# Bias rows of messages, projections and outputs: made by TensorE, or added by VectorE

## The chip, the cores and the metric

The kernel runs on one core of a Trainium2 chip. The metric is the device time of one execution in microseconds, and the times shown are medians of several runs. A core has five engines that run their own instruction streams and meet at semaphores: TensorE (PE; matmuls, with weight loads shown apart as PEld), VectorE (DVE), ScalarE (ACT), GpSimd (POOL) and SyncE (SP, which here issues most DMAs).

## The reference

Four graph layers run one after another over 1875 nodes of 256 features and 60000 edges, each with a residual sum and a layer norm: `x = layernorm(x + L(x))`. The first is a relational attention layer with 8 relations and 4 heads. The other three are where the change lies:

- The second layer has, for each of two relations, a two-step message per node, `m = relu(relu(x W_r + b_r) W_r + b_r)`, summed over the edges of that relation, and then one step of a recurrent cell and a three-layer network with biases `b1`, `b2`, `b3`.
- The third layer is two SAGE convolutions in a row. Each projects, `xp = relu(x W_proj + b_proj)`, averages `xp` over the incoming edges, and forms `out = aggr W_l + b_l + x W_r`, whose rows are divided by their norm. Between the two is a relu.
- The fourth is an attention layer with four heads that has no bias.

All is computed in float32.

## The kernel before

The 1875 nodes are held as 15 tiles of 128 rows, the features as 256 columns. The engines' programs are written out by hand, with semaphores named in the code; nothing is planned by a tool, so the order in the source is the order on each engine. The first 1126 us (the first layer) gather and sort edge data and walk over it; the rest is dense work.

Segment sums of messages are dense too: a matrix of edge counts, kept as 16-bit integers (`adjacency`), is cast by ScalarE and VectorE into chunks of float32 and multiplied by TensorE with the messages. To keep precision, a message is split into two halves: ScalarE writes the high half as `relu` of the PSUM bank (`message`, line 735), VectorE writes the low half as `max(bank, 0) - high` from the same bank (`low_half`, line 1360), and only then is the bank free.

A bias that varies along the columns is made by TensorE: the bias is split into three bf16 parts in three partitions (`bias_parts`, lines 1288 to 1305, seven VectorE instructions in a chain), and a matmul of three rows with a matrix of ones writes the bias row to all 128 partitions of the bank, before the matmuls of the data are accumulated on it. There are 105 such matmuls:

- Messages of the second layer (lines 1835 to 1837): ten groups of three tiles, in banks 4, 5 and 6. For each tile one bias matmul and two data matmuls (fp32; each is seen as two passes in the trace, so four passes a tile). Before each group but the first and the last stands the hidden layer of a later group (`hidden`, line 1812, eight passes of 384 columns). A group waits until the low halves of the group before are done (`m_ev`). ScalarE takes the hidden layer's relu (line 745) and the three high halves in turn.
- The last layer of the gate network (lines 1926, 1927): 15 bias matmuls. The bias parts of the next stage are made by VectorE in the second of the five gate rounds, between the statistics and the residual sum (line 1421).
- Projections (`project`, lines 1938 to 1940): 15 tiles for each convolution in four banks, `t % 4`; tile t waits for the low half of tile t - 4 (`p_ev`). The first four tiles of the second convolution are issued in the outputs' tail of the first. In front of the low halves of the second convolution VectorE computes the attention columns of the fourth layer (`attention_columns`, line 1446).
- Outputs (lines 1971 to 1974): 15 tiles for each convolution. For each tile two matmuls with `W_l` into the left half of a bank, one bias matmul and two matmuls with `W_r` into the right half. VectorE then scales the left half by the reciprocal count (line 1476), adds the right half (line 1477) and takes the sum of squares (line 1478). At the end of each group of four tiles it normalises; in the second convolution it also adds to `X` and computes the layer norm (lines 1489, 1309, 1322).

SyncE loads the first bias rows with the relation weights in the walk of the first layer (`first_weights`, line 478), into three partitions. It loads the bias rows of the convolutions when the relations' aggregation is done (line 518), and the six weights of the convolutions when the last matmul of the gate network is done (`x3_mm`, line 521). TensorE waits for all six before the first projection.

## Time and profile before

| | us |
|---|---|
| median of 3 runs | 1721.92 |
| lowest and highest | 1721.28, 1725.96 |
| profiled execution | 1728.33 |
| its span in the profile | 1726.6 |

| engine | busy us | share of the span | instructions |
|---|---|---|---|
| PE | 1377.2 | 80% | 4918 |
| PEld | 774.1 | 45% | 4918 |
| DVE | 1150.2 | 67% | 2944 |
| ACT | 725.8 | 42% | 1258 |
| POOL | 545.8 | 32% | 517 |

The profile is of one execution; times in it count from the start of its span. Busy time of PE is the sum of its matmuls' latencies as far as they don't overlap, so a busy PE need not be PE at its best. PEclk is the TensorE clock that was granted, as a share of full speed; the clock has two levels, 1.2 and 2.4 GHz, so a mean of 0.92 over a stretch means that 16% of it ran at the lower one. A row of the timeline gives the start, the time from the first instruction's start to the last one's end, the engine, the line of the code, what it does and how many instructions were merged; brackets say how long the engine had been idle and what ended the wait.

### The profile page before, as it was taken

Reading aid. Unit: us, or ns where it says so; the run is one execution under the profiler, and the core shown is the slowest. Engines: PE = TensorE matmul, PEld = TensorE weight load, DVE = VectorE, ACT = ScalarE, POOL = GpSimd, SP = SyncE. Lnnn points to the kernel's source line nnn. Section 1 sums busy time; section 2 is a strip of 40 time slices with the busy share of each in tenths; the row PEclk is TensorE's granted clock in tenths of the full one; section 3 lists DMA queues with packets and bytes.
Section 4 is the critical chain, followed back from the end, with each engine's and each line's share of the span. In section 5 each row is a group of like instructions: output and inputs, shape, how many; then the busy total and the mean of one; then the engine's idle time right before and its main releaser. Section 6 shows DMA issues by size and latency. Waiting matters only on the chain.

```text
span 1726.6 us, 21308 instructions
## 1 busy us (share of the span) xinstructions
PE 1377.2 (80%) x4918; PEld 774.1 (45%) x4918; DVE 1150.2 (67%) x2944; ACT 725.8 (42%) x1258; POOL 545.8 (32%) x517
## 2 busy tenths in 40 slices
PE   5897987777777777777169999979999989989930
PEld 2453643411111111112058777745876548758620
DVE  6232544289999999998989998852375443543737
ACT  1233543367777777776000000023595535316022
POOL 0102777777777777775000000000000000000023
PEclk9998555665555555555559999989999989989985
DMA  4534666765555565555148888600000010000023
GB/s 168 153 131 149 210 210 215 214 189 181 188 181 188 178 190 182 185 179 161 48 136 302 265 276 270 212 1 0 0 27 2 1 37 0 2 13 1 2 67 73
DMA packets 84505, 223.88 MB, mean 130 GB/s; under 512 B 18456, under 2 KB 27588, under 8 KB 83908
## 3 DMA queue, kind: packets, MB, share of 16 engines
q1 hardware_dynamic: 60452, 158.01, 26.4%
q0 software_dynamic: 23968, 64.77, 14.3%
q8 instruction: 50, 0.82, 0.2%
q14 instruction: 35, 0.29, 0.1%
HBM read 140.09 MB, written 82.63 MB: 129 GB/s over the span
## 4 chain that ended last, share of the span: by engine, by line
PE 48%; DVE 23%; issue 15%; POOL 6%; DMA 3%; ACT 3%; DVEq 2%; SPq 0%; POOLq 0%; ACTq 0%
PE bank L1786 13%; PE bank L1846 10%; PE bank L1645 6%; POOL arena L601 5%; DVE arena L1172 4%; DVE arena L1173 3%; DVE adjacency L1179 3%; PE bank L1901 2%; PE bank L1940 2%; DVE arena L1214 2%; PE bank L1837 2%; DVE arena L1391 2%; PE bank L1812 2%; PE bank L1974 1%; DVEq L404 1%
## 5 line engine op out<-in xcount | busy, mean ns | idle before, releaser
L601 POOL DMA_INDIRECT arena<-feat_table,arena x469 | 508.6, 1084 | 241.6 <-issue 228.8
L1725 PE MATMUL bank<-arena 128*128 128x480 f16 x586 | 336.1, 574 | 123.4 <-DVE arena L1173 116.5
L683 ACT ACTIVATE arena<-bank 128x480 uint16<-128x480 f32 x586 | 332.7, 572 | 119.1 <-PE bank L1725 112.5
L609 POOL DMA_INDIRECT arena<-al_table,edge_ends x15 | 14.7, 982 | 861.5 <-DMA al_table<-arena 857.2
L1179 DVE TENSOR_TENSOR adjacency<-adjacency,arena 128x480 uint16 x586 | 233.3, 398 | 10.2 <-DVE arena L1192 6.2
L1725 PEld LDWEIGHTS bank<-arena 128*128 128x128 f16 x586 | 60.9, 104 | 398.8 <-DVE arena L1173 307.1
L1786 PE MATMUL bank<-arena 128*128 x966 | 230.0, 393 | 0.8 <-issue 0.3
L1786 PEld LDWEIGHTS bank<-arena 128*128 128x128 f32 x966 | 175.4, 191 | 55.7 <-issue 33.7
L1173 DVE TENSOR_SCALAR arena<-iota,arena 128x480 f16<-128x480 f16 x586 | 196.5, 335 | 0.0
L1270 DVE TENSOR_TENSOR arena<-arena 128x1024 f32<-128x1024 f32 x118 | 139.8, 1212 | 14.6 <-DMA arena<-edge_rows 13.0
L1172 DVE TENSOR_SCALAR arena<-iota,arena 128x128 f16<-128x128 f16 x586 | 144.1, 246 | 0.8 <-ACT adjacency L647 0.8
L1645 PE MATMUL bank<-arena 128*128 128x512 f32 x240 | 111.2, 619 | 5.8 <-ACT arena L632 3.0
L1846 PE MATMUL bank<-count_chunks,message_halves 128*128 128x472 f32 x480 | 103.4, 377 | 2.1 <-DVE message_halves L1360 2.1
L715 ACT ACT_TABLE_LOAD x2 | 2.6, 1283 | 240.3 <-DVE ln_mean_var L1316 240.3
L1846 PEld LDWEIGHTS bank<-count_chunks,message_halves 128*128 128x128 f32 x480 | 90.0, 188 | 15.5 <-issue 2.9
L1688 PE MATMUL bank<-arena 128*128 x588 | 74.9, 189 | 16.4 <-DVE arena L1129 11.1
L781 ACT ACTIVATE count_chunks<-adjacency 128x944 fp32r<-128x944 uint16 (+1 forms) x30 | 69.9, 2334 | 39.7 <-PE bank L1846 39.7
L1688 PEld LDWEIGHTS bank<-arena 128*128 128x128 f16 x588 | 59.6, 105 | 46.4 <-issue 33.3
L1277 DVE TENSOR_TENSOR arena<-iota,arena 128x1024 f32<-128x1024 f16 (+1 forms) x61 | 73.7, 1209 | 9.2 <-PE bank L1786 8.8
L632 ACT ACTIVATE arena<-bank 128x512 f32<-128x512 f32 x60 | 35.8, 597 | 100.5 <-PE bank L1645 96.8
L1674 PE MATMUL bank<-adjacency,ident 128*128 128x512 f16 x128 | 66.3, 617 | 14.6 <-ACT arena L659 11.6
L1645 PEld LDWEIGHTS bank<-arena 128*128 128x128 f32 x240 | 46.9, 200 | 61.6 <-issue 54.4
(311 smaller groups left out, 1725.4 us busy)
## 6 DMA issues: line engine op xcount, KB each, us to landing
arena<-edge_rows SPq DMA_DIRECT2D x117, 520.0 KB, 4.5
edge_rows<-arena SPq DMA_DIRECT2D x67, 520.0 KB, 2.9
edge_rows<-arena SPq DMA_DIRECT2D x67, 390.0 KB, 2.6
feat_table<-arena SPq DMA_DIRECT2D x60, 260.0 KB, 2.1
arena<-feat_table,arena POOLq DMA_INDIRECT x469
arena<-in_w SPq DMA_DIRECT2D x1, 2048.0 KB, 9.8
arena<-in_xT SPq DMA_DIRECT2D x1, 1920.0 KB, 18.3
arena<-in_x SPq DMA_DIRECT2D x1, 1792.0 KB
```

Of the source, the lines that this page charges most:

```text
L601: g.indirect_dma_start(out=PLACE[k][:, t - lo, :], out_offset=None, in_=feat_t, in_offset=bass.IndirectOffsetOnAxis(ap=IE[:, t:t + 1], axi ...
L683: a.activation(EV[st % AS].rearrange("p r k -> p (r k)"), PS[4 + st % 4][:, 0:R2 * KW], ACT.Copy)\
L1172: v.tensor_scalar(OHS[st % AS], iota128[:, :], lo, None, ALU.is_equal)
L1173: v.tensor_scalar(OHK[st % AS], iota480[:, :], key, None, ALU.is_equal).then_inc(s["a_oh"], 1)
L1179: v.tensor_tensor(dst, dst, EV[st % AS], ALU.add).then_inc(s["a_add"], 1)
L1270: v.tensor_tensor(rows, rows, al, ALU.mult).then_inc(s["r_wgt"], 1)
L1277: v.tensor_tensor(OHR[:, i % ORING, 0:n * P].rearrange("p (s j) -> p s j", j=P), iota128[:, :].rearrange("p (a j) -> p a j", a=1).to_broad ...
L1645: ins = mm(PS[c][:, :], XT0[:, k, P * t:P * (t + 1)], W0[:, k, 512 * c:512 * (c + 1)], start=(k == 0), stop=(k == 1))
L1688: ins = mm(PS[4 + g % 2][:, 3 * H * k:3 * H * (k + 1)], KO[g % 3][:, lo:lo + P], ERW[:, bass.ds(offs[k], 3 * H)], start=True, stop=True)
L1725: mm(PS[4 + st % 4][:, 0:R2 * KW], OHS[st % AS], OHK[st % AS], start=True, stop=True).then_inc(s["a_mm"], 1)
L1786: mm(BANKS[:, bass.ds(out_at, D)], OHR[:, (st // RG) % ORING, P * (st % RG):P * (st % RG + 1)], FBf[:, bass.ds(places[st % RK] >> 12, D)], ...
L1846: ins = mm(PS[4 * fo + j0 + j][:, 0:CW], m[:, P * fo:P * (fo + 1)], ch[:, CW * j:CW * (j + 1)], start=start, stop=stop)
```

## The change

The 90 bias matmuls of messages, projections and outputs are left out; the first data matmul starts the accumulation. The bias rows are loaded by broadcast to all 128 partitions in float32. For messages and projections VectorE adds the bias to the bank in place (`add_bias`) as soon as TensorE has finished the tile and signals `biased`; ScalarE waits for that signal in place of TensorE's, and the low half follows as before. VectorE issues its adds ahead of the low half of the tile before. For outputs the bias goes into VectorE's first instruction, which scales the left half and adds the bias in one. The gate network keeps its bias matmuls, so `bias_parts` remains for that one row of 256 columns, and the splitting in the second gate round goes. The four bias rows of the convolutions (128 KB each now) are loaded ahead of the six weights; TensorE waits for all ten.

```diff
             def first_weights():
...
-                for i, b in enumerate((brow[0:1, :], brow[1:2, :], b3)):
-                    sp.dma_start(BROW[0][0:3, D * i:D * (i + 1)], b.broadcast_to([3, D])).then_inc(s["ld_wt1"], 16)
+                for b, to in ((brow[0:1, :], BIAS1[0]), (brow[1:2, :], BIAS1[1]), (b3, BROW[0:3, :])):
+                    sp.dma_start(to, b.broadcast_to([to.shape[0], D])).then_inc(s["ld_wt1"], 16)
...
-            sp.wait_ge(s["chunk_used"], R2 * SH)
-            for i, b in enumerate((bp1, bl1, bp2, bl2)):
-                sp.dma_start(BROW[1][0:3, D * i:D * (i + 1)], b.broadcast_to([3, D])).then_inc(s["ld_b2"], 16)
             sp.wait_ge(s["x3_mm"], NC)
+            for to, b in zip(BIAS2, (bp1, bl1, bp2, bl2)):
+                sp.dma_start(to, b.broadcast_to([P, D])).then_inc(s["ld_wt2"], 16)
             for i, w in enumerate((wp1, wl1, wr1, wp2, wl2, wr2)):
                 sp.dma_start(W2L[i], w.rearrange("(k p) n -> p k n", k=2)).then_inc(s["ld_wt2"], 16)
...
-            def message(n, bank, wide, exact=False):
+            def message(n, bank, wide, exact=False, before=0):
+                act.wait_ge(s["biased"], before + n + 1)
                 dst = WIDE[n] if wide else halves(n)[0] if exact else halves1(n)[0]
                 a.activation(dst, PS[bank][:, 0:D], ACT.Relu).then_inc(s["hi_ready"], 1)
...
+            def add_bias(bank, bias, made, count):
+                dve.wait_ge(made, count)
+                v.tensor_tensor(PS[bank][:, 0:D], PS[bank][:, 0:D], bias, ALU.add).then_inc(s["biased"], 1)
...
-                for n in range(R2 * NT):
-                    low_half(n, halves1(n), 4 + n % 3, s["m_ev"])
+                for n in range(0, R2 * NT, 3):
+                    for j in range(4):
+                        if j < 3:
+                            add_bias(4 + j, BIAS1[n // NT], s["m_mm"], n + j + 1)
+                        if j:
+                            low_half(n + j - 1, halves1(n + j - 1), 4 + j - 1, s["m_ev"])
...
-                if c == 1:
-                    dve.wait_ge(s["ld_b2"], 64)
-                    bias_parts(4, 1)
...
+                dve.wait_ge(s["ld_wt2"], 160)
                 with dve.If(large < 1):
-                    for t in range(NT):
-                        low_half(R2 * NT + u * NT + t, halves(t), t % 4, s["p_ev"])
+                    for t in range(NT + 1):
+                        if t < NT:
+                            add_bias(t % 4, BIAS2[2 * u], s["p_mm"], NT * u + t + 1)
+                        if t:
+                            low_half(R2 * NT + u * NT + t - 1, halves(t - 1), (t - 1) % 4, s["p_ev"])
...
-                        link(v.tensor_scalar(B1[:, t, :], PS[t % 4][:, 0:D], RC[:, t:t + 1], None, ALU.mult))
+                        link(v.scalar_tensor_tensor(B1[:, t, :], PS[t % 4][:, 0:D], RC[:, t:t + 1], BIAS2[1 + 2 * u], ALU.mult, ALU.add))
...
-                    mm(PS[4 + j][:, 0:D], ones16[0:3, :], BP[0:3, r, :], start=True, stop=False)
                     for k in range(2):
                         ins = mm(PS[4 + j][:, 0:D], HC[i % 2][:, k, P * j:P * (j + 1)], WREL[:, k, r, :],
-                                 start=False, stop=(k == 1))
+                                 start=(k == 0), stop=(k == 1))
...
-                mm(PS[t % 4][:, 0:D], ones16[0:3, :], BP2[0:3, 2 * u, :], start=True, stop=False)
...
-            pe.wait_ge(s["ld_wt2"], 96)
-            pe.wait_ge(s["bias_ready"], 2)
+            pe.wait_ge(s["ld_wt2"], 160)
...
-                    mm(PS[b][:, D:2 * D], ones16[0:3, :], BP2[0:3, 1 + 2 * u, :], start=True, stop=False)
```

## Rows read from the trace of the kernel before

**Rows 1.** Busy time by stage: stretch, length, busy us of engines (instructions), PEclk, DMA.

```profile
1150.60:1210.50 59.90, 58.88 (x214) 35.16 (x214) 12.30 (x29) 21.21 (x47) 0.00 (x0) 1.00 0.00 1
...
1406.30:1428.10 21.80, 20.75 (x76) 12.35 (x76) 6.36 (x15) 5.76 (x15) 0.00 (x0) 0.92 0.00 1
...
1482.30:1520.80 38.50, 37.87 (x160) 27.04 (x160) 25.35 (x80) 8.07 (x8) 0.00 (x0) 0.92 0.01 2
1520.80:1550.20 29.40, 23.84 (x82) 14.24 (x82) 11.66 (x30) 6.45 (x18) 0.00 (x0) 0.83 0.06 17
...
1604.40:1645.00 40.60, 38.91 (x162) 27.93 (x163) 32.57 (x112) 3.19 (x12) 0.00 (x0) 0.96 0.00 1
```

**Rows 2.** Groups by line from 1150 us: busy us, mean ns, idle before and releaser.

```profile
L1476 DVE TENSOR_SCALAR arena<-bank,recip_count 128x256 f32<-128x256 f32 x30 | 14.4, 481 | 17.4 <-PE bank L1974 17.4
...
L1477 DVE TENSOR_TENSOR arena<-arena,bank 128x256 f32<-128x256 f32 x30 | 12.6, 420 | 1.0
...
L1972 PE MATMUL bank<-arena,ones 3*128 3x256 bf16 x30 | 8.7, 289 | 0.0
L1835 PE MATMUL bank<-arena,ones 3*128 3x256 bf16 x30 | 8.3, 277 | 2.3 <-ACT arena L745 1.3 <-DVE last_messages L1360 1.0
...
L1489 DVE SCALAR_TENSOR_TENSOR arena<-arena,ln_rstd 128x256 f32<-128x256 f32 x15 | 6.3, 480 | 0.1
```

**Rows 3.** Timeline of the message stage: one tile, a hidden layer, a low half.

```profile
1158.25 0.28 PE L1835 MATMUL bank<-arena,ones 3*128 3x256 bf16 x1
...
1158.46 1.13 PE L1837 MATMUL bank<-arena 128*128 128x256 f32 x4
...
1159.52 0.28 PE L1835 MATMUL bank<-arena,ones 3*128 3x256 bf16 x1
...
1160.70 2.74 PE L1812 MATMUL bank<-arena 128*128 128x384 f32 x8
...
1161.31 0.42 DVE L1360 SCALAR_TENSOR_TENSOR first_messages<-bank,first_messages 128x256 fp32r<-128x256 f32 x1 [0.85 <-ACT first_messages L735]
...
1163.37 0.28 PE L1835 MATMUL bank<-arena,ones 3*128 3x256 bf16 x1
```

**Rows 4.** Timeline of the attention tiles, which have no bias: ScalarE's evictions.

```profile
1655.06 0.39 ACT L835 ACTIVATE arena<-bank 128x264 f32<-128x264 f32 x1 [0.50 <-PE bank L1951]
1655.95 0.39 ACT L835 ACTIVATE arena<-bank 128x264 f32<-128x264 f32 x1 [0.50 <-PE bank L1951]
```

**Rows 5.** Timeline of the second gate round: VectorE after the splitting.

```profile
1360.35 0.69 DVE L1428 TENSOR_TENSOR arena<-arena,bank 128x512 f32<-128x512 f32 x1 [0.47 <-PE bank L1927]
```

**Rows 6.** Timeline before the first projection: weight loads, TensorE's wait.

```profile
1398.22 0.41 SPq L521 DMA_DIRECT2D arena<-in_wp  x1
...
1400.71 0.48 SPq L521 DMA_DIRECT2D arena<-in_wr  x1
...
1406.29 0.28 PE L1938 MATMUL bank<-arena,ones 3*128 3x256 bf16 x1 [2.08 <-DMA arena<-in_wr]
```

**Rows 7.** DMA issues: KB each, median us from issue to landing.

```profile
arena<-in_a3l SPq DMA_DIRECT2D x1, 128.0 KB, 3.1
arena<-in_a3r SPq DMA_DIRECT2D x1, 128.0 KB, 3.6
```

**Rows 8.** Timeline, start of the first convolution's aggregation.

```profile
1428.07 4.12 PE L1846 MATMUL bank<-count_chunks,message_halves 128*128 128x472 f32 x18 [1.05 <-DVE message_halves L1360]
```

**Rows 9.** Timeline of the second projection, behind the attention columns.

```profile
1530.61 1.40 DVE L1360 SCALAR_TENSOR_TENSOR message_halves<-bank,message_halves 128x256 fp32r<-128x256 f32 x4
1531.08 0.39 PE L1938 MATMUL bank<-arena,ones 3*128 3x256 bf16 x1 [4.51 <-DVE message_halves L1360]
```

**Rows 10.** Timeline of the second outputs, VectorE: in the first group and later.

```profile
1612.69 0.48 DVE L1476 TENSOR_SCALAR arena<-bank,recip_count 128x256 f32<-128x256 f32 x1 [0.73 <-PE bank L1974]
...
1632.70 0.48 DVE L1476 TENSOR_SCALAR arena<-bank,recip_count 128x256 f32<-128x256 f32 x1
...
1634.02 0.48 DVE L1476 TENSOR_SCALAR arena<-bank,recip_count 128x256 f32<-128x256 f32 x1
```

More of the change, by code:

```diff
@@ L374, in build @@
         TMP3 = ar(A_WT + 1040, D)
-        BROW = [ar(A_BI, 4 * D), ar(A_CH + 10 * D, 4 * D)]
-        BPF = [AR[:, A_BI + 2 * D * j:A_BI + 2 * D * (j + 1)].bitcast(BF16) for j in range(2)]
-        BP, BP2 = (f.rearrange("p (b n) -> p b n", n=D) for f in BPF)
-        BSPLIT = [[AR[:, o + 2 * D * j:o + 2 * D * (j + 1)].bitcast(BF16) for j in range(3)] + [AR[:, o + 6 * D:o + (10 - k) * D]]
-                  for k, o in ((1, A_WT + 1024), (0, A_CH))]
+        BROW, BPF = ar(A_WT + 1024 + 5 * D // 2, D), AR[:, A_BI + D:A_BI + 3 * D // 2].bitcast(BF16)
+        BSPLIT = [AR[:, A_WT + 1024 + D // 2 * j:A_WT + 1024 + D // 2 * (j + 1)].bitcast(BF16) for j in range(3)]\
+            + [ar(A_WT + 1024 + 3 * D // 2, D)]
+        BIAS1 = [ar(A_BI, D), REM]
+        BIAS2 = [ar(A_BI + D * j, D) for j in range(4)]
         GT = ar(A_B1, 6, CN)
@@ L387, in build @@
             var_ready std_ready ln_done xt_mm xt_eva xt_evd h_mm h_ev m_mm m_ev chunk_ready cast_act cast_dve first_half_used chunk_half chunk_used agg_eva
-            agg_evd gate_mm gate_ev c_ready tc_ready hn_ready x1_mm x1_ev x2_mm x2_ev x3_mm x3_add ld_b2 ld_wt2 ld_wt3
+            agg_evd gate_mm gate_ev c_ready tc_ready hn_ready x1_mm x1_ev x2_mm x2_ev x3_mm x3_add biased ld_wt2 ld_wt3
             p_mm p_ev hi_ready cnt_red cnt_mm big_mm o_mm o_ready nrm_done h_ready pool_gate vl3_done t_mm t_ev t_st key_mm
@@ L814, in _ @@
                 if c in (2, 3):
-                    act.wait_ge(s["bias_ready"], 2)
+                    act.wait_ge(s["cnt_mm"], 1)
                     early_cast(0, c - 2)
@@ L839, in messages2 @@
                     for t in range(NT):
-                        act.wait_ge(s["p_mm"], NT * v + t + 1)
-                        message(t, t % 4, wide, True)
+                        message(t, t % 4, wide, True, R2 * NT + NT * v)
                     for c in range(2, SH):
@@ L1290, in _, with last_bias_parts @@
                     weigh(b)
-            def bias_parts(n, k):
-                row = lambda ap: ap[0:3, 0:n * D]
+            def last_bias_parts():
+                row = lambda ap: ap[0:3, 0:D]
                 part = lambda q: ident[0:3, q:q + 1]
-                hi, mid, lo, rem = BSPLIT[k]
-                link(v.tensor_copy(row(hi), row(BROW[k])))
-                link(v.tensor_tensor(row(rem), row(BROW[k]), row(hi), ALU.subtract))
+                hi, mid, lo, rem = BSPLIT
+                link(v.tensor_copy(row(hi), row(BROW)))
+                link(v.tensor_tensor(row(rem), row(BROW), row(hi), ALU.subtract))
                 link(v.tensor_copy(row(mid), row(rem)))
                 link(v.tensor_tensor(row(lo), row(rem), row(mid), ALU.subtract))
-                link(v.tensor_scalar(row(BPF[k]), row(hi), part(0), None, ALU.mult))
-                link(v.scalar_tensor_tensor(row(BPF[k]), row(mid), part(1), row(BPF[k]), ALU.mult, ALU.add))
-                v.scalar_tensor_tensor(row(BPF[k]), row(lo), part(2), row(BPF[k]), ALU.mult, ALU.add).then_inc(s["bias_ready"], 1)
-                dve.wait_ge(s["bias_ready"], k + 1)
+                link(v.tensor_scalar(row(BPF), row(hi), part(0), None, ALU.mult))
+                link(v.scalar_tensor_tensor(row(BPF), row(mid), part(1), row(BPF), ALU.mult, ALU.add))
+                v.scalar_tensor_tensor(row(BPF), row(lo), part(2), row(BPF), ALU.mult, ALU.add).then_inc(s["bias_ready"], 1)
+                dve.wait_ge(s["bias_ready"], 1)
             def stats(t0, t1):
@@ L1334, in _ @@
             dve.wait_ge(s["ld_wt1"], 16 * 5)
-            bias_parts(3, 0)
+            last_bias_parts()
             dve.wait_ge(s["flag_ready"], 2)
@@ L1376, in _ @@
                 for n in range(R2 * NT):
+                    add_bias(4 + n % 3, BIAS1[n // NT], s["m_mm"], n + 1)
                     no_rest(n, s["m_ev"])
@@ L1468, in _ @@
                     for t in range(NT):
+                        add_bias(t % 4, BIAS2[2 * u], s["p_mm"], NT * u + t + 1)
                         dve.wait_ge(s["hi_ready"], R2 * NT + u * NT + t + 1)
@@ L1925, in _ @@
                     o = PS[6 + j // 2][:, D * (j % 2):D * (j % 2 + 1)]
-                    mm(o, ones16[0:3, :], BP[0:3, 2, :], start=True, stop=False)
+                    mm(o, ones16[0:3, :], BPF[0:3, :], start=True, stop=False)
                     ins = mm(o, X2[:, P * j:P * (j + 1)], W3s, start=False, stop=True)
@@ L1937, in project @@
                     xt_ready(u + 1, max(1 - u, t // 4))
-                mm(PS[t % 4][:, 0:D], ones16[0:3, :], BP2[0:3, 2 * u, :], start=True, stop=False)
                 for k in range(2):
-                    ins = mm(PS[t % 4][:, 0:D], XT[:, k, P * t:P * (t + 1)], W2L[3 * u][:, k, :], start=False, stop=(k == 1))
+                    ins = mm(PS[t % 4][:, 0:D], XT[:, k, P * t:P * (t + 1)], W2L[3 * u][:, k, :], start=(k == 0), stop=(k == 1))
                 ins.then_inc(s["p_mm"], 1)
@@ L1971, in _ @@
                         mm(PS[b][:, 0:D], B2T[:, k, P * t:P * (t + 1)], Wl[:, k, :], start=(k == 0), stop=(k == 1))
[L1972 removed]
                     for k in range(2):
[L1974 removed]
+                        ins = mm(PS[b][:, D:2 * D], XT[:, k, P * t:P * (t + 1)], Wr[:, k, :], start=(k == 0), stop=(k == 1))
                     ins.then_inc(s["o_mm"], 1)
```

2 lines of the change are left out of this document (removed).

## The prediction, made before the changed kernel was run

> **What bounds the kernel now.** I read the busy shares of the page first, then a table by stage, then single tiles. The page alone misleads: the change touches nothing before 1100 us (indirect gathers, the walk over edges), except that two small loads grow. Of the last 576 us five stages hold bias matmuls that go [rows 1]: relation messages, first projection, first outputs, second projection, second outputs, in the order of the windows. In the first three windows TensorE is busy for 58.9 of 59.9, 20.8 of 21.8 and 37.9 of 38.5 us, VectorE for 12.3, 6.4 and 25.4: TensorE sets the pace and VectorE has room. The fourth has a stall, the fifth (1604.4) is VectorE's for most of its length.
>
> **What a bias row costs TensorE.** 90 of 105 bias matmuls go: 30 in messages (L1835), 30 in projections, 30 in outputs (L1972) [rows 2]; the 15 of the last layer of the gate network stay. Their mean of 277 to 289 ns is a latency, not the price. A message tile repeats every 1.27 us: bias at 1158.25, weights' matmuls from 1158.46, next bias at 1159.52 [rows 3]. So the bias holds 0.21 us by itself and the four fp32 passes 1.06. What would four such passes take without a bias among them? The attention tiles have none: four passes of 264 columns, and ScalarE gets one each 0.89 us (1655.06, 1655.95) [rows 4]; 256 columns make 0.86. So a bias row costs 0.21 of its own and 0.20 that its switch of operand type adds around it: 1.27 - 0.86 = 0.41 us a tile. Bounds: 0.21 and 0.41. I take 0.41, since the attention tile is the same operation at the same clock.
>
> **Messages.** 30 x 0.41 = 12.3 us gone, if TensorE stays the bound. Each group of three tiles is followed by eight passes for the next hidden layer, 1160.70 to 1163.37, 2.67 us [rows 3]. The third tile's low half ends at 1161.73, 1.64 us before TensorE wants the banks. Now a tile goes TensorE, VectorE add, ScalarE, VectorE low half; the third add waits also behind the first low half. No row shows VectorE writing PSUM. Nearest rows: a two-operand pass with one in PSUM, L1477, 0.42; one with a pointer scalar, L1489, 0.48 [rows 2]; below, four low halves in a row take 1.40, 0.35 each [rows 9]; above, a pass to read and one to write, 0.84. I take 0.42, as L1477 reads the same operands. With 0.42 and some 0.07 of hand-over the third low half ends about 0.5 later: 1.1 us of cover remain. VectorE then works 6 x 0.42 = 2.5 us of a 5.15 us period. The cover lacks twice: before the tenth group, which no hidden layer precedes, and at the end, before the first count chunk is cast. 2 x 0.45 = 0.9. Messages: -11.4 (bounds -5 and -11.9).
>
> **Aggregations and gates.** Nothing in them changes but that VectorE drops seven splitting instructions of 1024 columns in the second gate round. They ended 0.47 us before TensorE's last result of that round [rows 5], so they were hidden: 0. The splitting before the first layer norm shrinks to a third, also in a wait. The two broadcasts to all partitions there go past SyncE's queue of row blocks and put 256 KB before the block that VectorE already waits for; TensorE has over 1 us in hand there. 0, at most +1.
>
> **The loads before the first projection.** The four bias rows were loaded during earlier stages, into three partitions. Now they go to 128 partitions and stand on SyncE ahead of the six weights, all after the last gate matmul; TensorE waits for all ten (160). Before: six issues from 1398.22, the last at 1400.71, TensorE starts at 1406.29 after 2.08 us of waiting [rows 6]. Four more issues at 0.51 are 2.0 us, the lower bound. The same kind of load is there later: two broadcasts of 128 KB, issued 0.51 apart, land after 3.1 and 3.6 us [rows 7], so the second takes 1.0 us more, 131 GB/s; four of them are 4.0 us, the upper bound if weights don't overlap them. I take +3.0. The Trainium skill ("DMA: Bandwidth & Descriptors", section "Anatomy of one DMA — SWDGE (gpsimd) path") has a transfer cost its bytes at 436 GB/s beside a fixed part; by that, an estimate, 512 KB are 1.2 us, the issues would be the bound and the sum 1 us better. The rows of a broadcast show less than a third of that rate.
>
> **First projection.** 15 tiles, four banks. VectorE has two passes a tile, 0.70 to 0.84 us, below TensorE's 0.86; TensorE barely stays the bound. The clock: 0.92 over 21.8 us is 3.5 us at the lower level [rows 1]. I let that stretch stay as long: at half clock a tile takes 1.72, two tiles; the other 13 take 0.86, in sum 14.7 in place of 20.7 (1406.29 to about 1427). -6.0, less 0.5 for the add in the tail before the aggregation, which already waits 1.05 for the last low half [rows 8]. I round to -5.3, since VectorE is so near.
>
> **First outputs.** The bias add is folded into VectorE's first pass, a tensor_scalar of 0.48 [rows 10] that becomes a scalar_tensor_tensor with a pointer scalar, also 0.48 (L1489) [rows 2]: 0. TensorE: a tile comes each 2.13 us (VectorE starts at 1612.69 after waiting 0.73; the second output stage begins as the first) and loses 0.41. VectorE needs 1.32 a tile when it waits for nothing (1632.70 to 1634.02) [rows 10], below 1.72. 15 x 0.41 = 6.1. VectorE's 25.4 us [rows 1] would still fit in the 32.4 that remain. -6.1.
>
> **Second projection.** Its first four tiles run in front of the attention columns: 4 x 0.41 = 1.6. Then TensorE waits 4.51 us, because VectorE does the attention columns before its first low half at 1530.61 [rows 9]. ScalarE had all four messages done by then; now it must wait for VectorE's add, so the first bank comes free one add, one message and the hand-overs later: +1.0 (bounds 0.8 and 1.4). The 11 tiles after it took 18.0; with 9.5 us at half clock (0.83 over 29.4 us is 10.0 [rows 1]) 5.5 tiles fall in that and 5.5 take 0.86: 14.2, -3.8. Tail +0.5. Sum -3.9.
>
> **Second outputs.** Only the first group waits for TensorE [rows 10]; later VectorE runs without a gap, and its work is unchanged. 4 x 0.41: -1.6. The attention stage behind it moves along.
>
> **Sum.** -11.4 + 3.0 - 5.3 - 6.1 - 3.9 - 1.6 = -25.3 us. The profiled execution took 1728.3 (span 1726.6): 1703.0. It was 6.4 above the median of 1721.92; the stages are the same in both, so I take the difference from the median: 1696.6, about 1697 us.
>
> **Rivals.**
> (a) A bias row gives back only its own 0.21: the gap around it belongs to the weight loads of 0.19 us each and stays. Then messages -5.4, first projection -3.1 + 0.5, outputs -3.1, second projection -0.8 - 2.3 + 1.5, outputs -0.8, loads +3.0: -10.5, 1711 us. Against it: attention tiles have the same weight loads. 0.14.
> (b) VectorE becomes the bound of the projections: the in-place add takes 0.84, a tile 1.26. Some 18.5 tiles at full clock lose 0.40, +7.4, and four tails and the join 0.4 each, +2: 1706 us. 0.17.
> (c) Slower than before: TensorE now waits a little for VectorE at each tile, and the clock stays low through projections and outputs. At half clock throughout, the projections take 25.8 (+5.1) and 18.9 behind the join (+0.9, and +2 before it), the outputs 15 x 3.44 = 51.6 (+13.1) and, where that exceeds VectorE, +11; with -11.4, +3.0 and +1.5 this is +25, 1747 us. It decides from about 50 us more at the lower level on, half of which is the 25 gained. Against it: in messages TensorE has a gap at each type switch and the window reads 1.00 [rows 1]. The Trainium skill ("TensorE: Matmul & The Clock Gate", section "A second HAM failure mode: psum-queue depth-cycling") describes such a fall from short idles between groups that cycle through banks; no window here shows it without a stall of over 2 us ahead. 0.04.
> (d) The loads cost 8 us rather than 3, since 128 copies of one row are read from one place: 1702. 0.06.
> That it doesn't do what it says (the matmuls stay the bound with no gain, same time): 0.03.
>
> **How the numbers follow.** Forecast 0.56: 1690 to 1703 (clock stretches of the four restarts, each some 2 us either way, loads 2 to 4). With (a), (b) and (d) the range is 1688 to 1712, which leaves the far side of (a), (c) and a gain above 34 us out. A measurement tells 0.3%, 5.2 us, from no change. Faster: forecast, (a), (b), (d) = 0.93; same: 0.03; slower: 0.04.
>
> **What would show it.** Messages: groups of three 5.15 us apart rather than 6.39; at 5.76, (a) holds. The window of messages at clock 1.00. In-place adds of about 0.42 us; at 0.8, (b). First projection starting 10.1 to 12.1 us after the first of SyncE's issues rather than 8.1, its tiles 0.86 apart at full clock. Output tiles of 1.72 in the first stage; the second no more than 2.5 us shorter. The stall behind the attention columns about 1 us longer. The forecast is wrong if messages gain under 8 us or if the clock shares fall below 0.8 outside the stall.

## The result, and the profile after

The changed kernel takes 1698.66 us (median of 4 runs, 1697.88 to 1698.85) beside 1722.06 for the kernel before on the same chip (4 runs, 1721.28 to 1725.96): ratio 0.9858, 95% interval 0.9838 to 0.9879, 23.4 us less. Two further sets, on other chips, gave 0.9853 (0.9835 to 0.9872) and 0.9872 (0.9849 to 0.9895). The forecast was 1697, its range 1688 to 1712. The profiled execution took 1697.88 us (span 1695.8).

The first view is the table by stage: stretch, length, busy us of PE, PEld, DVE, ACT and POOL, granted clock, DMA share, GB/s. The stages are messages, first projection, first outputs, second projection, second outputs; the first one runs on to the aggregation's start, where [rows 1] end at the last message. The same stretch of the kernel before is the first line; the other five are the changed kernel's.

```profile
1150.60:1212.79 62.19, 58.88 (x215) 35.17 (x215) 13.65 (x31) 23.46 (x50) 0.00 (x0) 1.00 0.00 1
```
```profile
1150.27:1201.52 51.25, 47.02 (x184) 34.81 (x184) 24.61 (x61) 23.43 (x50) 0.00 (x0) 1.00 0.00 1
1398.09:1414.95 16.86, 15.34 (x60) 12.87 (x61) 11.43 (x30) 5.75 (x15) 0.00 (x0) 0.87 0.01 1
1469.15:1499.01 29.86, 28.79 (x144) 25.33 (x145) 24.75 (x80) 8.17 (x8) 0.00 (x0) 1.00 0.03 8
1499.01:1521.46 22.45, 15.55 (x67) 13.00 (x67) 16.82 (x45) 6.86 (x18) 0.00 (x0) 0.92 0.05 15
1575.64:1614.70 39.06, 34.84 (x146) 29.16 (x147) 32.54 (x112) 3.17 (x12) 0.00 (x0) 0.91 0.00 1
```

Against that line and [rows 1] all five are shorter: messages by 10.9 us, then by 4.9, 8.6, 7.0 and 1.5. The granted clock differs too (0.92, 0.92 and 0.83 before in the three stages of the middle, 0.96 in the last), and that part is not the change's arithmetic, as the experiments show.

The timeline of the message stage, TensorE and then VectorE, answers to [rows 3]; the columns are start, length, engine, line, operation, and in brackets the idle time before and its releaser.

```profile
1155.52 2.75 PE L1845 MATMUL bank<-arena 128*128 128x256 f32 x12
1158.11 2.74 PE L1821 MATMUL bank<-arena 128*128 128x384 f32 x8
1160.69 2.75 PE L1845 MATMUL bank<-arena 128*128 128x256 f32 x12
```
```profile
1158.31 0.43 DVE L1362 TENSOR_TENSOR bank<-bank,arena 128x256 f32<-128x256 f32 x1
1158.65 0.96 DVE L1357 SCALAR_TENSOR_TENSOR first_messages<-bank,first_messages 128x256 fp32r<-128x256 f32 x2
```

Three tiles are now one run of twelve passes: 1155.52 to 1158.11, 2.59 us, 0.86 a tile against 1.27. The group repeats after 5.17 us. The third addition starts at 1158.31, the last low half ends at 1159.61, and TensorE wants the bank at 1160.69: 1.1 us of cover.

The groups by line (busy us, mean ns, idle before and its releaser) have the new operations, beside [rows 2]:

```profile
L1362 DVE TENSOR_TENSOR bank<-bank,arena 128x256 f32<-128x256 f32 x60 | 25.8, 431 | 37.5 <-PE bank L1845 24.5 <-PE bank L1947 9.7
L1485 DVE SCALAR_TENSOR_TENSOR arena<-bank,recip_count,arena 128x256 f32<-128x256 f32 x30 | 14.4, 480 | 7.8 <-PE bank L1979 7.8
```

The addition in PSUM takes 431 ns. The outputs' first pass takes 480, as the 481 of the operation that it replaces, and waits 7.8 us for TensorE where that one waited 17.4.

The timeline around the loads answers to [rows 6] (SPq is SyncE's queue): the first bias row, the first weight, the first projection; then the aggregation's start [rows 8] and the stall of the second projection [rows 9].

```profile
1387.08 0.33 SPq L518 DMA_DIRECT2D arena<-in_bp  x1
...
1388.88 0.43 SPq L520 DMA_DIRECT2D arena<-in_wp  x1
```
```profile
1398.09 15.34 PE L1947 MATMUL bank<-arena 128*128 128x256 f32 x60 [5.02 <-DMA arena<-in_wr]
1414.95 1.33 PE L1854 MATMUL bank<-count_chunks,message_halves 128*128 128x472 f32 x5 [1.52 <-DVE message_halves L1357]
...
1508.78 3.40 PE L1947 MATMUL bank<-arena 128*128 128x256 f32 x8 [5.39 <-DVE message_halves L1357]
```

From the first issue to the projection it is 11.0 us where it was 8.1; the wait for each of the two aggregations grew from 1.05 to 1.5, the stall from 4.51 to 5.39. These are the prices; together they are 4.8 us, a fifth of the 23.4 gained.

### The profile page after: what moved, and what is told of

Same layout as the page of the kernel before. It is cut to its first block, busy times and chain, and to the rows that moved or that the text cites. A ratio compares the mean times of both kernels' runs of the same rounds, so it can differ in the third digit from the quotient of the medians.

```text
span 1695.8 us, 21179 instructions
## 1 busy us (share of the span) xinstructions
PE 1338.8 (79%) x4828; PEld 772.0 (46%) x4828; DVE 1161.1 (68%) x2997; ACT 726.1 (43%) x1258; POOL 545.6 (32%) x517
## 4 chain that ended last, share of the span: by engine, by line
PE 45%; DVE 24%; issue 16%; POOL 6%; DMA 3%; ACT 3%; DVEq 2%; SPq 0%; POOLq 0%; ACTq 0%
PE bank L1795 14%; PE bank L1854 10%; PE bank L1654 6%; POOL arena L600 5%; DVE arena L1170 4%; DVE arena L1171 3%; DVE adjacency L1177 3%; PE bank L1909 2%; DVE arena L1212 2%; PE bank L1947 2%; DVE arena L1398 2%; PE bank L1821 2%; PE bank L1845 2%; DMA arena<-feat_table,arena 1%; DVEq L404 1%
## 5 line engine op out<-in xcount | busy, mean ns | idle before, releaser
L1795 PEld LDWEIGHTS bank<-arena 128*128 128x128 f32 x966 | 175.0, 191 | 57.0 <-issue 35.5
```

What stands on the lines that cost most here:

```text
L1795: mm(BANKS[:, bass.ds(out_at, D)], OHR[:, (st // RG) % ORING, P * (st % RG):P * (st % RG + 1)], FBf[:, bass.ds(places[st % RK] >> 12, D)], ...
```

## The experiments

**Both kernels profiled once more.** The profiled pair differs by 30.5 us, the medians by 23.4. Neither kernel was edited here.

> The kernel before once more, nothing edited, to see how far its stages vary between two profiled executions. Theory: the first profiled execution of before lay 6.3 us above its median because TensorE stayed at 1.2 GHz longer in two stretches (first outputs, granted clock 0.92 over 38.51 us; second projection, 0.83 over 29.41 us); a second look shows 1721 to 1724 us, and the two stretches are together 4 to 8 us shorter at a higher granted clock, with messages (62.2 us), aggregations (54.2 us) and the first projection (21.8 us) within 0.5 us of the first look. Rival: those 6 us belong to the kernel before in every execution and the profiled one is slow elsewhere (under 2 us between the looks in these two stretches).

> The changed kernel once more, nothing edited. Theory: 1697.9 to 1699 us, 0.984 to 0.988 of before; stretches that begin right after a stall of TensorE (first outputs 29.86 us, second projection 22.45 us, second outputs 36.96 us) may move by 1 to 3 us with their granted clock, the full-clock ones (messages 51.25 us, aggregations 54.2 us) by under 0.3 us. Rival: the stages repeat to 0.3 us each, the clock included.

Before took 1727.48 us in its second profiled execution, the set's other runs 1720.45 to 1727.6 with a median of 1722.58. The changed kernel: 1698.62 (1697.6 to 1699.27). The same table for the second profile of before (first projection, first outputs, second projection), then for that of the changed kernel:

```profile
1406.13:1430.94 24.81, 23.77 (x75) 13.61 (x76) 6.36 (x15) 5.75 (x15) 0.00 (x0) 0.79 0.00 1
1485.15:1522.28 37.13, 36.50 (x160) 26.34 (x160) 25.34 (x80) 8.12 (x8) 0.00 (x0) 0.95 0.01 1
1522.28:1549.29 27.01, 21.45 (x82) 12.91 (x82) 11.66 (x30) 6.47 (x18) 0.00 (x0) 0.94 0.06 19
```
```profile
1398.77:1415.44 16.67, 15.16 (x60) 12.66 (x61) 11.43 (x30) 5.76 (x15) 0.00 (x0) 0.88 0.01 1
1469.62:1501.16 31.54, 30.48 (x145) 26.49 (x145) 24.74 (x80) 8.13 (x8) 0.00 (x0) 0.95 0.02 5
1501.16:1524.39 23.23, 16.32 (x67) 13.51 (x67) 16.81 (x45) 6.87 (x18) 0.00 (x0) 0.85 0.06 17
```

The theory of the first text missed its numbers: 1727.48 us where 1721 to 1724 was expected, a first projection that moved by 3.0 us where 0.5 was allowed, and the two other stretches 3.8 us shorter where 4 to 8 was expected. What holds of it is that messages repeat to 0.03 us and the aggregations to 0.02, while the stages behind a stall move by up to 3 us, and their granted clock moves with them: what the outputs and the second projection won (3.8 us) the first projection gave back (3.0). I take it that the surplus of before's profiled executions over its median lies in whichever stages start at the lower clock. The other runs have no stages, so this is inferred, but their clock agrees: of 17 in the last set, the three with a mean granted clock of 0.764 over the whole span took 1717.86 to 1719.56 us, the three with 0.759 took 1727.08 to 1728.21 (between them the order is not strict). The changed kernel kept to its theory, and its rival falls.

Length times granted clock takes that out where TensorE is busy throughout: the first projection is 20.0 and 19.6 in the two profiles before, 14.7 and 14.7 after; the first outputs are 35.4 and 35.3, then 29.9 and 30.0. In the second projection and the second outputs TensorE also stands still, and a wait doesn't go with the clock (the stall is 5.39 us in all three profiles of the changed kernel), so there the product is rough: for the second projection it is 24.4 and 25.4 before, 20.7 and 19.8 after. Why both profiles of before fell at the slow end of its runs stays open; stages are compared below by that product where the clock differs.

**The rows put back, stage by stage.** Each returned matmul is thrown away, VectorE's additions stay. First the messages, then the 60 tiles of the projections and outputs of both convolutions.

```diff
                 for j in range(3):
+                    mm(PS[4 + j][:, 0:D], ones16[0:3, :], BPF[0:3, :], start=True, stop=True)
                     for k in range(2):
```

> The changed kernel with one bias matmul per message tile issued on PE again ahead of the data, its result thrown away (the next matmul starts the bank anew); VectorE's additions stay. It prices the messages' part by itself: 30 rows on PE. Theory (PE sets the pace there, a row between fp32 passes costs 0.41 us a tile): a group of three goes from 5.17 to about 6.4 us, +11 to +12.3 us over the changed kernel: 1709.5 to 1711 us. Rival 1 (VectorE, with only 1.1 us of cover a group, had become the pace after the change, so that a row on PE is partly hidden): +3 to +8 us. Rival 2 (a row costs its own 0.21 us alone, and the rest of the messages' gain came from another change in order): +6.3 us.

1711.7 us (1708.97 to 1716.05, 6 runs), ratio 0.9929 (0.9911 to 0.9947): 13.1 above the changed kernel's 1698.62 in the same set. The message stage of this kernel:

```profile
1151.14:1214.24 63.10, 58.88 (x214) 35.16 (x214) 24.58 (x61) 23.48 (x50) 0.00 (x0) 1.00 0.00 1
```
```profile
1158.79 0.28 PE L1844 MATMUL bank<-arena,ones 3*128 3x256 bf16 x1
1159.00 1.13 PE L1846 MATMUL bank<-arena 128*128 128x256 f32 x4
1160.06 0.28 PE L1844 MATMUL bank<-arena,ones 3*128 3x256 bf16 x1
```

A tile is 1.27 us again, the stage 11.85 longer, as the theory has it (30 x 0.41 = 12.3, less some 0.4 in the first and the tenth group, which start behind a wait of TensorE and hide part of a row's price); both rivals fall. The median is 0.7 us above the expected range. The other 1.3 of the 13.1 us are outside the stage; in the profiles the granted clock of the stretch up to the loads varies from 0.94 to 0.97 between kernels that run the same instructions there.

```diff
+                mm(PS[t % 4][:, 0:D], ones16[0:3, :], ident[0:3, :].bitcast(BF16), start=True, stop=True)
                 for k in range(2):
                     ins = mm(PS[t % 4][:, 0:D], XT[:, k, P * t:P * (t + 1)], W2L[3 * u][:, k, :], ...
...
+                    mm(PS[b][:, D:2 * D], ones16[0:3, :], ident[0:3, :].bitcast(BF16), start=True, stop=True)
                     for k in range(2):
                         ins = mm(PS[b][:, D:2 * D], XT[:, k, P * t:P * (t + 1)], Wr[:, k, :], ...
```

> The changed kernel with one bias matmul per tile back on PE in both projections and both outputs of the second convolution (60 rows), each thrown away by the matmul after it; VectorE's work stays as changed. Theory (the medians are right, the profiled pair shows 7 us too much): the sum of the four predicted terms less what VectorE now binds, +13 to +17 us over the changed kernel: 1712 to 1716 us. Rival 1 (the stage differences of the profiled pair, 4.9 + 8.7 + 7.0 + 1.5, all belong to the rows): +21 to +23 us. Rival 2 (VectorE has become the bound in projections and outputs, rows on PE are mostly hidden): +3 to +9 us.

1718.78 us (1715.78 to 1720.41, 7 runs), ratio 0.9966 (0.9952 to 0.998): +20.2, above the theory's 13 to 17 and just under rival 1's 21 to 23. The intervals of the two ratios (0.9835 to 0.9872 for the changed kernel) have room for either. First projection, first outputs, second projection and second outputs (these up to the attention's first matmul), and the last of them in the second profile of the changed kernel:

```profile
1399.10:1422.92 23.82, 22.30 (x76) 13.04 (x76) 11.43 (x30) 5.76 (x15) 0.00 (x0) 0.85 0.00 1
1478.69:1514.23 35.54, 34.91 (x160) 25.43 (x160) 25.35 (x80) 8.14 (x8) 0.00 (x0) 1.00 0.01 1
1514.23:1544.16 29.93, 23.02 (x81) 13.75 (x82) 16.81 (x45) 6.86 (x18) 0.00 (x0) 0.83 0.05 17
1598.35:1631.71 33.36, 33.27 (x144) 23.88 (x145) 27.14 (x92) 2.00 (x7) 0.00 (x0) 1.00 0.00 0
```
```profile
1578.58:1610.77 32.19, 29.10 (x128) 24.86 (x129) 27.60 (x94) 2.00 (x7) 0.00 (x0) 0.95 0.00 1
```

Length times granted clock, this kernel less the second profile of the changed one: first projection 20.2 - 14.7, first outputs 35.5 - 30.0, second projection 24.8 - 19.7, second outputs 33.4 - 30.6, in sum 19.0 us (the last two are rough, for the reason above). So the expected range was missed. I worked it out anew after the result: VectorE's additions stay in this kernel, so the gross sizes of the prediction's terms count, without the tails and the join: 5.8 + 6.1 + 5.4 + 1.6 = 18.9. That the expectation was mis-worked and the terms hold rests on this sum by stage, not on the median. Rival 2 falls. Rival 1 is near in the median and is not excluded by it; against it stands that its numbers came from lengths with an unequal clock in them. The timeline of the first projection shows what that does, first in this kernel, then in the changed one:

```profile
1399.10 0.39 PE L1946 MATMUL bank<-ident,ones 3*128 3x256 bf16 x1 [4.95 <-DMA arena<-in_wr]
1399.42 2.08 PE L1948 MATMUL bank<-arena 128*128 128x256 f32 x4
1401.43 0.39 PE L1946 MATMUL bank<-ident,ones 3*128 3x256 bf16 x1
```
```profile
1400.20 0.43 DVE L1362 TENSOR_TENSOR bank<-bank,arena 128x256 f32<-128x256 f32 x1 [6.54 <-PE bank L1947]
1401.91 0.43 DVE L1362 TENSOR_TENSOR bank<-bank,arena 128x256 f32<-128x256 f32 x1 [1.28 <-PE bank L1947]
```

A tile at the lower clock takes 2.33 us with its row; in the changed kernel the first two additions, each of which waits for its tile, start 1.71 apart. There a row costs 0.62, not 0.41.

**Rows grouped, in the kernel before.** Same rows, a third of the changes of operand type.

```diff
+                for j in range(3):
                     mm(PS[4 + j][:, 0:D], ones16[0:3, :], BP[0:3, r, :], start=True, stop=False)
+                for j in range(3):
                     for k in range(2):
```

> The kernel before with the three bias matmuls of each message group issued one behind the other ahead of the group's twelve fp32 passes, in place of one ahead of each tile's four: 30 rows as before, a third of the changes between bf16 and fp32 matmuls. Theory (of the 0.41 us that a row costs, 0.21 is its own and 0.20 comes with the changes around it): the group's tiles take 3.1 to 3.4 us in place of 3.81, 10 groups, 4.2 to 7.2 us under before. Rival (the 0.20 belongs to each bias row, as its weight load or its own start): the group's tiles stay at 3.8 us, within 0.7 us of before by the stage.

```profile
1152.44 0.50 PE L1835 MATMUL bank<-arena,ones 3*128 3x256 bf16 x3
1152.87 2.86 PE L1838 MATMUL bank<-arena 128*128 128x256 f32 x12
1155.56 2.74 PE L1812 MATMUL bank<-arena 128*128 128x384 f32 x8
1158.24 0.50 PE L1835 MATMUL bank<-arena,ones 3*128 3x256 bf16 x3
```
```profile
1146.66:1202.86 56.20, 52.91 (x214) 36.15 (x214) 13.64 (x31) 23.43 (x50) 0.00 (x0) 1.00 0.00 1
```

The group repeats after 5.80 us (6.39 before, 5.17 without rows), the three tiles take 3.12, the stage 56.20 in place of 62.19: -6.0, inside the theory's range; the rival falls. Three rows cost 3 x (own + change) = 1.22 apart and 3 x own + change = 0.63 together, so a row's own share is 0.11 us and the change from fp32 to bf16 and back 0.30. The timeline agrees on the own share: from the first row to the fp32 passes it is 0.43 us with three rows and 0.21 with one, 0.11 for each further row. What in the change costs the time is not shown: the rows differ from their neighbours in operand type and also in shape (3 partitions against 128), and no run separates the two. By the medians, 1719.46 beside 1722.64 (0.9979, 0.9966 to 0.9992), only 3.2 of the 6.0 arrive; before's 17 runs in that set spread over 10 us, so I don't read more into it.

**Without the additions.** What VectorE's new work costs (the bias of messages and projections is left out).

```diff
                 dve.wait_ge(made, count)
-                v.tensor_tensor(PS[bank][:, 0:D], PS[bank][:, 0:D], bias, ALU.add).then_inc(s["biased"], 1)
+                dve.sem_inc(s["biased"], 1)
```

> The changed kernel without VectorE's 60 additions in PSUM (the bias of messages and projections is left out of the result; the outputs keep theirs): what the added VectorE work costs. Theory (off the path but for the tails: 0.47 us ahead of the tenth message group, 0.47 ahead of each of three aggregations, about 0.8 to 1.3 in the second projection's stall): 2.5 to 3.5 us under the changed kernel. Rival 1 (a read and write of a bank by VectorE beside PE's writes slows PE's matmuls too): 6 us or more under it, with message groups shorter than 5.17 us. Rival 2 (hidden altogether): within 1 us.

> The changed kernel, nothing edited, timed beside the next two on one chip, so that they are compared with it there. Both theories: 0.983 to 0.988 of before; messages 51.2 us and aggregations 54.2 us again; the first projection, outputs and second projection within 1 to 3 us of the two looks so far, by how long they run at the lower clock.

1695.95 us (1695.34 to 1699.15) beside 1698.9 (1698.01 to 1703.19) for the changed kernel in that set: 2.95 less, as the theory has it, though the intervals of the two ratios overlap (0.9827 to 0.9869, 0.9849 to 0.9895). The timeline shows the two tails of the messages, the waits ahead of the tenth group and of the aggregation:

```profile
1198.61 2.83 PE L1845 MATMUL bank<-arena 128*128 128x256 f32 x12 [1.08 <-DVE last_messages L1357]
1203.78 1.56 PE L1854 MATMUL bank<-count_half,first_messages 128*128 128x472 f32 x6 [2.34 <-ACT count_half L758]
```

With the additions they are 1.49 and 2.75, 0.41 more each; the waits ahead of the two later aggregations differ by as much (1.11 and 1.52), and the stall of the second projection is 4.76 us in place of 5.39. That is 2.3 us by the rows, so rival 2 falls too. The groups still repeat after 5.17 us, so additions in PSUM don't slow the matmuls beside them, and rival 1 falls. The changed kernel's third profile, in the same set, had its stages behind stalls within 2 us of the other two.

**A second pass.** How much room VectorE has in the projections; the added result is discarded.

```diff
+                            dve.wait_ge(s["p_mm"], NT * u + t + 1)
+                            v.tensor_tensor(PS[t % 4][:, D:2 * D], PS[t % 4][:, 0:D], BIAS2[2 * u], ALU.add)
                             add_bias(t % 4, BIAS2[2 * u], s["p_mm"], NT * u + t + 1)
```

> The changed kernel with one more addition by VectorE per projection tile (128x256, read and written in PSUM, thrown away by the outputs that follow), 30 in all: what VectorE's room in the projections is. Theory (VectorE's add, low half, add chain of 0.86 us a tile is already level with PE's 0.86): each addition costs its start-to-start time of 0.34 to 0.43 us wherever PE waits for buffers, +0.34 to 0.43 times 11 to 15 tiles in each projection, +7.5 to +11 us over the changed kernel: 1706 to 1710 us. Rival (VectorE still has 0.3 us a tile of room): under +3 us, from the tails of the two projections alone.

1706.3 us (1701.76 to 1709.65, 5 runs), ratio 0.9885 (0.9857 to 0.9913). On the chip of this run and of the next three the changed kernel was not timed. Against its medians on other chips that is some +7.5, at the theory's lower end; by the ratios to before (0.9853 to 0.9872 there) it is 2 to 5.5, with intervals that overlap. So the rows have to decide, and they show another reason than the theory's. Three passes in a row in the first projection, then the two projections by the table:

```profile
1408.26 0.42 DVE L1472 TENSOR_TENSOR bank<-bank,arena 128x256 f32<-128x256 f32 x1
1408.59 0.42 DVE L1362 TENSOR_TENSOR bank<-bank,arena 128x256 f32<-128x256 f32 x1
1408.92 0.41 DVE L1357 SCALAR_TENSOR_TENSOR message_halves<-bank,message_halves 128x256 fp32r<-128x256 f32 x1
1409.25 0.42 DVE L1472 TENSOR_TENSOR bank<-bank,arena 128x256 f32<-128x256 f32 x1
```
```profile
1402.26:1420.99 18.73, 16.21 (x61) 12.21 (x61) 15.29 (x45) 5.76 (x15) 0.00 (x0) 0.89 0.00 1
1506.55:1532.14 25.59, 17.25 (x66) 13.77 (x67) 21.04 (x60) 6.92 (x18) 0.00 (x0) 0.87 0.04 13
```

VectorE is without idle time there and sets the pace, at 0.99 us a tile: three passes start 0.33 apart. So two passes are 0.67 of TensorE's 0.86, with 0.19 of room, and the tile grew by 0.13 rather than 0.34: neither the theory's room of nothing nor the rival's 0.3. The two projections are 1.9 and 3.1 us longer than in the changed kernel's first profile; the rest of the median is again in stages that were not touched (1202.40 to 1402.26 took 199.9 us where the changed kernel had 196.6, 196.7 and 198.4, at a granted clock of 0.94 in place of 0.96 to 0.97).

**Bias rows loaded early, attention columns late, and both.**

```diff
+            sp.wait_ge(s["chunk_used"], R2 * SH)
+            for to, b in ((BIAS2[0], bp1), (BIAS2[2], bp2), (BIAS2[3], bl2)):
+                sp.dma_start(to, b.broadcast_to([P, D])).then_inc(s["ld_hb"], 16)
             sp.wait_ge(s["x3_mm"], NC)
-            for to, b in zip(BIAS2, (bp1, bl1, bp2, bl2)):
-                sp.dma_start(to, b.broadcast_to([P, D])).then_inc(s["ld_wt2"], 16)
...
+            sp.dma_start(BIAS2[1], bl1.broadcast_to([P, D])).then_inc(s["ld_xt"], 16)
...
-            pe.wait_ge(s["ld_wt2"], 160)
+            pe.wait_ge(s["ld_wt2"], 96)
```

> The changed kernel with three of the four copied bias rows of the second convolution loaded right after the relations' aggregation, long before their use, and the fourth (bl1, whose place is still in use then) queued behind the weights; PE waits for the six weights alone, VectorE for the rows. Theory (the copies take the DMA queue ahead of the weights and delay the first projection by 2.9 us): the stretch from the first weight's issue to the first projection falls from 11.0 to about 8.1 us, 2.4 to 3 us under the changed kernel: 1695.6 to 1696.3 us. Rival 1 (the weights alone, at the rate that they had, set that stretch, and the copies only lay beside them): within 0.7 us of 1698.6. Rival 2 (the freed time returns as a longer stretch at 1.2 GHz behind it): the stretch is shorter by 2.4 to 3 us and the whole by under 1.5.

1693.71 us (1690.95 to 1698.43), ratio 0.9828 (0.9799 to 0.9856). TensorE's wait, and the first projection by the table:

```profile
1393.31 8.90 PE L1950 MATMUL bank<-arena 128*128 128x256 f32 x40 [1.69 <-DMA arena<-in_wr]
```
```profile
1393.31:1408.04 14.73, 13.21 (x61) 11.32 (x61) 11.44 (x30) 5.76 (x15) 0.00 (x0) 1.00 0.00 1
```

The first weight is issued at 1385.63, the projection starts 7.7 us later, 3.3 less than with the copies ahead where 2.4 to 3 was expected, so rival 1 falls. Rival 2 came out the other way round: the stage behind is shorter too, 14.73 us at 1.00, 2 under the changed kernel. The moved bytes tell the same in a view of 1300 to 1402 us in 40 slices of 2.55 us (GB/s, changed kernel, then this one): the first two slices with the copies ahead show 58 and 107, the first two with weights alone 267 and 326.

```profile
GB/s 0 0 3 6 6 0 0 0 0 6 0 0 0 0 0 0 0 0 0 0 0 0 0 6 0 0 0 0 0 0 0 0 0 0 58 107 292 353 16 3
```
```profile
GB/s 0 3 0 6 43 108 10 0 6 0 0 0 0 0 0 0 0 0 0 0 0 0 6 0 0 0 0 0 0 0 0 0 0 2 267 326 80 0 0 0
```

```diff
-                if u == 1:
-                    attention_columns()
                 dve.wait_ge(s["ld_wt2"], 160)
...
                     second_halves(u, True)
+                if u == 1:
+                    attention_columns()
```

> The changed kernel with VectorE's attention columns moved from ahead of the second projection's additions to behind its aggregation's start, so that the additions of the four prefilled tiles don't queue behind them. Theory (PE's 5.4 us stall in the second projection is VectorE standing in the columns, 3.6 us of it, and not the additions themselves): the stall falls to about 1.7 us, 3.2 to 3.8 us under the changed kernel, 1694.8 to 1695.4, and up to 2 less where the shorter stall also shortens the stretch at 1.2 GHz. Rival 1 (the additions and low halves of four tiles need the time anyway): the stall stays above 4 us, the whole within 1 us. Rival 2 (the columns come late for the attention at the end, or hold up the eviction of the aggregate): the stall falls, the whole is unchanged or slower by 1 to 4 us.

1692.27 us (1690.74 to 1697.04), ratio 0.982 (0.9793 to 0.9847). The stall, against 5.39:

```profile
1503.21 9.08 PE L1947 MATMUL bank<-arena 128*128 128x256 f32 x33 [1.86 <-DVE message_halves L1357]
```

It fell by 3.5 us to near the 1.7 expected, and the second projection is 19.21 us. The median is 0.5 us below the expected range with all it allowed for the clock. Rivals 1 and 2 fall: the second aggregation kept its 54.2 us and the end its length.

> Both of the preceding edits in one kernel: bias rows loaded early, attention columns late. Theory: the two stretches don't touch, so the gains add, 5.6 to 6.8 us under the changed kernel, 1691.8 to 1693 us, up to 2 less with less time at 1.2 GHz. Rival (the clock takes back what a stall gives): under 4 us.

> The kernel with the early bias rows and the late attention columns once more, beside the changed kernel on the same chip. Theory: 7 to 10 us under the changed kernel (3.2 to 3.9 us at the loads, 2 at the first projection, which ran at 1.00 of the full clock in both kernels with early rows, 3 to 4 in the second projection), 1689 to 1692 us; the interval of its ratio to before ends under the changed kernel's. Rival (part of what the last runs showed was that chip's): 2 to 5 us under it.

1689.47 us (1686.73 to 1691.15; 0.9794, 0.9768 to 0.982), and in the other set 1688.75 (1687.39 to 1695.49; 0.982, 0.9795 to 0.9845), there 10.15 under the changed kernel (0.9872, 0.9849 to 0.9895), just above the expected 7 to 10; the rival falls. The gains add, and exceed the first text's sum; the profiles put this down to the clock: in the second set's both projections ran at 1.00 throughout.

```profile
1395.83:1410.56 14.73, 13.22 (x60) 11.32 (x61) 11.42 (x30) 5.75 (x15) 0.00 (x0) 1.00 0.01 1
1496.31:1513.83 17.52, 14.14 (x66) 11.96 (x67) 13.43 (x37) 6.85 (x18) 0.00 (x0) 1.00 0.08 20
```

This is the fastest version measured. The late columns don't need the change, though they were not tried in the kernel before; the early rows undo its largest price.

## Why the prediction was right, step by step

- **A row's price, 0.41 us a tile.** Right: tiles of 0.86 after, 1.27 with the row back. Its split into 0.21 own and 0.20 around was wrong; it is 0.11 and 0.30 (what the 0.30 belongs to, type or shape, stays open). The sum doesn't hang on it, but rival (a) does: by its own share alone, messages would have gained 3 us.
- **Messages, -11.4.** -10.9. The addition (0.42 taken, 0.43 measured), the cover (1.1) and the tails (0.45 taken, 0.41 to 0.47) all hold; some 0.4 of the missing 0.5 is the part of the rows' price that the first and the tenth group hid behind their waits.
- **Aggregations and gates, 0.** From the aggregation's start (1212.79 before) to SyncE's first issue it was 185.4 us [rows 6] and is 185.6.
- **Loads, +3.0.** The 8.1 us became 11.0. Of these 2.9 us 1.8 pass before SyncE issues its first weight (1387.08 to 1388.88), near the lower bound of 2.0 for four more issues; the other 1.1 come behind that issue, so the rate of the copies is at most the smaller part. The Trainium skill's figure ("DMA: Bandwidth & Descriptors", section "Anatomy of one DMA — SWDGE (gpsimd) path") would have given +2.0, though that section is on transfers that GpSimd issues and these are SyncE's; the 2.9 measured and the slices at 58 and 107 GB/s decide against it for copies of one row.
- **First projection, -5.3.** -4.9 in the first pair, -8.1 in the second, -5.1 by length times granted clock. VectorE has more room than "barely", 0.19 us a tile; rival (b) fails on 0.43, and on a start-to-start of 0.33.
- **First outputs, -6.1.** -8.6 and -5.6; by length times clock -5.4. The fold into the first pass costs nothing (480 against 481 ns).
- **Second projection, -3.9.** -7.0 and -3.8, by length times clock -4.7 (24.9 to 20.2, means of two profiles, a rough product here). The stall grew by 0.9 as forecast (+1.0).
- **Second outputs, -1.6.** -1.5 in the stretch of the table at a lower clock than before (0.91 against 0.96). From the stage's start to the kernel's end, 122.2 us in both profiles before, it is 120.2, 118.6 and 118.8 after. Both profiles before and the first one after begin the stage partly at the lower clock (0.57, 0.68 and 0.61 over its first 4 us): that pair gives -2.0, near the term. The two others after begin it at 1.00, and there the sign "no more than 2.5 us shorter" failed, by the clock.
- **The sum.** -25.3, taken from the profiled execution and then from the median, gave 1696.6; the medians moved by 23.4, so the forecast was 1.7 to 2.1 us low. To carry before's surplus over as a constant ("the stages are the same in both") was the right choice for the median, but its reason was wrong, so that landing within 2.1 us is in part luck: the surplus, as far as the runs tell, is time at the lower clock, which the changed kernel's profiled executions don't have (0.8 us under their median, 0.3 above, 0.8 under). Hence the profiled pairs differ by 30.5 and 28.5, more than the change is worth. Term by term, at equal clock, the stages give -10.9 + 2.9 - 5.1 - 5.4 - 4.7 - 2.0 = -25.2 us: messages, first projection and first outputs were taken 0.2 to 0.7 us too large, the second projection and the second outputs 0.8 and 0.4 too small. That the medians moved by 1 to 2 us less is not placed in a stage; a candidate is the 2 us at the lower clock behind the copies, which went away with the early rows.

The single experiments come near to closing the account by medians: rows of the messages 13.1 and of the second part 20.2, less 2.95 for the additions and 4.9 for the copies ahead of the weights (this one between two chips), make 25.5 beside the 23.4 to 24.0 measured. Rival (c), slower by a lost clock, didn't come: in the changed kernel's three profiles no stage of the five fell under 0.85, and messages stayed at 1.00 as before [rows 1]. The fall of the clock from short idles that the Trainium skill describes ("TensorE: Matmul & The Clock Gate", section "A second HAM failure mode: psum-queue depth-cycling") shows in no message stage of any run here: they ran at 0.99 to 1.00.

## What to carry to other kernels

A small matmul of another operand type and shape between fp32 matmuls was paid here mostly at the two changes: compare the period of the same tile with and without it, not its duration; group such rows if they must stay, and take them to an idle engine if it has the cover. Whatever the engine then needs (here rows copied to all partitions) has to be loaded in an earlier stage, not right ahead of the critical loads in the same queue. Where a stage starts behind a stall, give its term as length times granted clock with a separate allowance for the waits in it, and profile two executions before reading 3 us from one.

## What the runs showed that I had not expected

- A bf16 matmul of 3x256 costs 0.11 us next to its like and 0.30 for the change from the fp32 passes of 128 partitions and back; at the lower clock the row costs 0.62 in all.
- VectorE passes of 128x256 with an operand in PSUM last 0.42 us in the trace, and start 0.33 apart when nothing holds them, an addition that writes its own bank too.
- The first projection of kernels without its rows ran at 1.00 in three executions where TensorE had waited 1.4 to 1.7 us for weights, and at 0.83 to 0.89 in seven where it had waited 4.6 to 5.2. So shortening a stall paid twice (early rows: 3.3 us at the loads and 2 behind). But with the rows in place a wait of 1.7 (grouped rows) was followed by 0.90, and waits of 2.08 and 1.75 (before) by 0.92 and 0.79, so the length of the wait alone doesn't decide, and I can't say what else does.
- The kernel before spread over 10 us within a set (1717.86 to 1728.21, 1718.03 to 1728.7), roughly in step with its mean granted clock: as much as the messages' term.
